# GpSimd splits the attention weights in the middle of the expert loop: a drain between two of its instructions becomes a wait on the first one's semaphore

## The chip, the cores and the metric

One core of a Trainium2 chip runs the whole program. The metric is the device time of one execution in microseconds (us); lower is better. The profile's names are PE (TensorE), DVE (VectorE), ACT (ScalarE), POOL (GpSimd) and SP (SyncE); an engine name with a small q (POOLq) is that engine's sequencer, which carries out waits, semaphore increments and drains.

## The reference, cut to what matters

The input is 4 sequences of 1024 tokens with 512 features. Three layers follow one another:

```
x = x + 0.5 * ffn(layernorm(x))      # 32 routed experts, top 6, capacity 192, plus one shared expert
x = x + attention(layernorm(x))      # 4 query heads on 1 key/value head of 128, causal, rotary
x = x + 0.5 * ffn(layernorm(x))      # the same weights again
```

An expert gathers its 192 tokens, computes `silu(x Wg) * (x Wu)`, multiplies by `Wd` (inner width 256), weights each row and adds the rows back to their tokens. Products are made to fp32 accuracy from two parts of each factor: hi is the value cast to fp32r, lo is value minus hi. The attention layer needs its weights `w_qkv` (512 x 768) and `w_out` (512 x 512) in this form too. They are split while the experts of the first ffn run, and that splitting is what the change touches.

## The kernel before, in words

`ffn(0)`, `attention` and `ffn(1)` run one after the other. Inside an ffn, `front` does the normalisation, shared expert and routing; `routed_experts` then loops over the 32 experts with everything double buffered (`u = e % 2`). No planner orders the expert loop: each engine has its own list of instructions, written out by hand, and semaphores tie the lists together.

For expert e the work passes through the engines like this:

- SP loads the expert's weights `e_raw` (1.5 MB) as soon as the buffer is free, that is when DVE has finished the lo part of expert e-2 (L881 in the first half, L890 in a loop).
- POOL gathers the expert's tokens with two indirect DMAs, `gather`, L898 (`e_xg` from the table `htab`).
- PE turns the tokens (L1100), which waits for the gathers to land. It then computes gate and up (L1111, L1112) and down (L87 to L89). It turns expert e+2 before it computes gate and up of e+1.
- ACT casts the weights to `e_w_hi` (L958), unloads PSUM, and writes the weighted result `e_y` in `weigh` (L987 and L990). `weigh` of expert e waits until `y_free` has reached e+1.
- DVE subtracts `e_w_lo` (L1032) and does the other lo parts and sums.
- POOL adds the result rows into the output with two indirect DMAs, `scatter`, L909. The scatter of an expert waits for its `e_y`, and for `added`, which says that all earlier scatters have landed. It increments `y_free` (L906) before it issues.

POOL issues all of this from one list. For each index e it runs `gather_next(e)`, which waits for `col_done` and gathers the tokens of expert e+2, and then the scatter of expert e-2. In the first ffn, for the ten indices e = 4 to 13, a `split_chunk` stands between them:

```
for e in range(4, 4 + chunks):
    gather_next(e // 2, e % 2)
    split_chunk(e - 4)
    scatter(e // 2 - 1, e % 2)
```

A chunk is 128 x 512 fp32 (256 KB). `attention_chunks` lists six of `w_qkv` and four of `w_out`. The first six are loaded by SP before the expert loop, and the other four are loaded by L885 behind the expert weights. Chunk c waits for its load, is cast to hi (L915), the drain follows (L916), and the subtraction gives lo (L917). The second ffn has the same loop without chunks.

Of the kernel before, what the change touches and what calls it, by code (L numbers as in the profile page):

```python
# [31 lines left out]
XS = 6  # L32
# [63 lines left out]
def own_semaphore(nc, k, name):  # L96

    k.ffn_semaphores.append(nc.alloc_semaphore(name=name))
    return k.ffn_semaphores[-1]
# [720 lines left out]
def routed_experts(nc, a, k, n, htab, acc, slots, raw, xs, w_loaded, y_stored):  # L820

    with ExitStack() as ctx:
        sb = lambda name, shape, dt: ctx.enter_context(nc.sbuf_tensor(f"{name}{n}", shape, dt))
        pb = lambda name: ctx.enter_context(nc.psum_tensor(f"{name}{n}", [P, 512], F32))
        sem = lambda name: own_semaphore(nc, k, f"{name}{n}")
# [29 lines left out]
        d_ready, y_ready = sem("e_d_ready"), sem("e_y_ready")  # L855
        part = lambda t, c, m: t[:, 2 * c:2 * c + 2, m, :]
        if n == 0:
            att_loaded, att_split = [sem(f"e_att_loaded{u}_") for u in range(XS)], sem("e_att_split")
            cut = lambda ap, c: ap.rearrange("p k c -> p (k c)")[:, c * D:(c + 1) * D]
            attention_chunks = [tuple(cut(ap, c) for ap in (hi[:, :, :], lo[:, :, :], from_))  # L860
                                for hi, lo, from_, size in ((k.wqkv_hi, k.wqkv_lo, a["w_qkv"], WQKV),
                                                            (k.wo_hi, k.wo_lo, a["w_out"], H * D))
                                for c in range(size // D)]
# [4 lines left out]
        with nc.Block() as block:  # L868

            @block.sync  # L870
            def _(sp):
                if n == 0:
                    for c, (hi, lo, from_) in enumerate(attention_chunks):
                        if c < XS:
                            sp.wait_ge(y_stored[c], 16 * ((NT - 1 - c) // XS + 1))
                            sp.dma_start(xs[c][:, :], from_).then_inc(att_loaded[c], 16)
                for i in range(E // 4):
                    for u in range(2):
                        e = 2 * i + u
                        sp.wait_ge(lo_ready, 3 * e + 3)  # L880
                        sp.dma_start(raw[u][:, :], a["w_experts"][e + 2, :, :]).then_inc(w_loaded[u], 16)  # L881
                        if n == 0 and XS <= e - 4 + XS - 1 < len(attention_chunks):
                            c = e - 4 + XS - 1
                            sp.wait_ge(att_split, c - XS + 1)
                            sp.dma_start(xs[c % XS][:, :], attention_chunks[c][2]).then_inc(att_loaded[c % XS], 16)  # L885
                with sp.Fori(E // 4, E // 2 - 1) as i:
                    for u in range(2):
                        e = 2 * i + u
                        sp.wait_ge(lo_ready, 3 * e + 3)
                        sp.dma_start(raw[u][:, :], a["w_experts"][bass.ds(e + 2, 1), :, :].rearrange("o p c -> p (o c)")).then_inc(w_loaded[u], 16)  # L890

            @block.gpsimd
            def _(pool):
                pool.sem_inc(y_free, 2)

                def gather(u):
                    for q in range(2):
                        pool.indirect_dma_start(xg[u][q][:, :], None, htab,  # L898
                                                bass.IndirectOffsetOnAxis(ap=gather_idx[u][:, q:q + 1], axis=0)).then_inc(gathered[u], 16)

                def scatter(i, u, first=False):
                    e = 2 * i + u
                    pool.wait_ge(y_ready, 2 * e + 2 + 2)
                    if not first:
                        pool.wait_ge(added, 32 * e)
                        pool.sem_inc(y_free, 1)  # L906
                    pool.sem_inc(seen, 1)  # L907
                    for q in range(2):
                        pool.indirect_dma_start(acc, bass.IndirectOffsetOnAxis(ap=add_idx[u][:, q:q + 1], axis=0),  # L909
                                                y[u][q][:, :], None, compute_op=ALU.add).then_inc(added, 16)  # L910

                def split_chunk(c):
                    hi, lo, from_ = attention_chunks[c]
                    pool.wait_ge(att_loaded[c % XS], 16 * (c // XS) + 16)
                    pool.tensor_copy(hi, xs[c % XS][:, :])  # L915
                    pool.drain()  # L916
                    pool.tensor_tensor(lo, xs[c % XS][:, :], hi.bitcast(F32), ALU.subtract).then_inc(att_split, 1)  # L917

                def gather_next(i, u):
                    pool.wait_ge(col_done, 2 * i + u + 1)  # L920
                    pool.sem_inc(seen, 1)
                    gather(u)

                for u in range(2):
                    pool.tensor_copy(gather_idx[u][:, :], slots[:, 2 * u:2 * u + 2])
                pool.drain()
                gather(0)
                gather(1)
                gather_next(0, 0)
                gather_next(0, 1)  # L930
                for u in range(XS):
                    pool.wait_ge(y_stored[u], 16 * ((NT - 1 - u) // XS + 1))
                gather_next(1, 0)
                scatter(0, 0, first=True)
                gather_next(1, 1)
                scatter(0, 1)
                chunks = len(attention_chunks) if n == 0 else 0
# [4 lines that stand above are left out]
                with pool.Fori((4 + chunks) // 2, E // 2 - 1) as i:  # L942
                    for u in range(2):
                        gather_next(i, u)
                        scatter(i - 1, u)
                for i in (E // 2 - 2, E // 2 - 1):
                    for u in range(2):
                        scatter(i, u)
                pool.wait_ge(added, 32 * E)
# [716 lines left out]
def build_program(nc, a, out):  # L1666
    with ExitStack() as ctx:
        k = allocate_kept(nc, ctx)
        htab = nc.dram_tensor("htab", [ROWS, ROW], F32).ap()
        x1 = nc.dram_tensor("x_after_ffn", [ROWS, D], F32).ap()  # L1670
        x2 = nc.dram_tensor("x_after_attention", [TOK, D], F32).ap()

        def ffn(n, src, acc):
            with nc.sbuf_tensor(f"slots{n}", [HALF, 2 * E + 4], U32) as slots, ExitStack() as places:
                staged = [staged_buffers(nc, places, "place", PLACES - 2 + u, n) for u in range(2)]
                raw = [nc.alloc_sbuf_tensor_at(f"e_raw{u}_{n}", [P, WALL], F32, offset=staged[u][0]) for u in range(2)]
                xs = [places.enter_context(nc.sbuf_tensor(f"d_xs{u}_{n}", [P, D], F32)) for u in range(XS)]
                w_loaded = [own_semaphore(nc, k, f"e_w_loaded{u}_{n}") for u in range(2)]
                y_stored = [own_semaphore(nc, k, f"d_y_stored{u}_{n}") for u in range(XS)]
                front(nc, a, k, n, src, acc, (x1, out), htab, slots, staged, raw, xs, w_loaded, y_stored)  # L1680
                routed_experts(nc, a, k, n, htab, acc, slots, raw, xs, w_loaded, y_stored)

        ffn(0, a["x"], x1)
        attention(nc, a, k, x1, x2)
        ffn(1, x2, out)
# [72 lines left out]
```

## Time and profile before

| quantity | value |
|---|---|
| time, median of 3 runs | 1744.37 us (1742.22 to 1751.76) |
| profiled execution: own time | 1754.33 us |
| profiled execution: span | 1752.5 us |
| mean granted TensorE clock, share of full speed | 0.945 |
| PE, DVE, ACT, POOL busy, share of the span | 86%, 64%, 59%, 45% |

The span is the profiler's time from first to last instruction; the execution's own time is 1.8 us longer. The shares are averages over stages that are limited by different things, so the stage in which the change stands has to be read by itself. The expert loop of the first ffn lies between about 219 us and 600 us of the span, with the ten chunks between 271.7 and 408.3 us.

### The profile page before, as it was taken

Reading aid. Unit: us, or ns where it says so; the run is one execution under the profiler, and the core shown is the slowest. Engines: PE = TensorE matmul, PEld = TensorE weight load, DVE = VectorE, ACT = ScalarE, POOL = GpSimd, SP = SyncE. Lnnn points to the kernel's source line nnn. Section 1 sums busy time; section 2 is a strip of 40 time slices with the busy share of each in tenths; the row PEclk is TensorE's granted clock in tenths of the full one; section 3 lists DMA queues with packets and bytes.
Section 4 is the critical chain, followed back from the end, with each engine's and each line's share of the span. In section 5 each row is a group of like instructions: output and inputs, shape, how many; then the busy total and the mean of one; then the engine's idle time right before and its main releaser. Section 6 shows DMA issues by size and latency. Waiting matters only on the chain. (4 is left out here: it accounts for less than half of the span.)

```text
span 1752.5 us, 26196 instructions
## 1 busy us (share of the span) xinstructions
PE 1508.2 (86%) x8434; PEld 1255.1 (72%) x8436; DVE 1113.4 (64%) x2274; ACT 1027.8 (59%) x2098; POOL 788.7 (45%) x679
## 2 busy tenths in 40 slices
PE   5999867777899278999999999986999969999994
PEld 4877766666787266887888788774777758787773
DVE  5669756445677236676766676664558867777773
ACT  5852346445677237666766766653763437777773
POOL 0113145555555266656665556520113234565553
PEclk9999979888999779999999999998999989999998
DMA  7745467656898410111111111103664447999994
GB/s 263 253 126 174 121 197 224 175 163 184 240 263 247 74 48 25 53 45 46 40 37 61 49 37 37 43 30 112 228 217 137 145 139 225 258 262 259 258 258 78
DMA packets 94597, 255.57 MB, mean 146 GB/s; under 512 B 19152, under 2 KB 20112, under 8 KB 86192
## 3 DMA queue, kind: packets, MB, share of 16 engines
q1 hardware_dynamic: 71984, 202.58, 34.4%
q0 software_dynamic: 22528, 51.92, 14.6%
q8 instruction: 45, 0.74, 0.2%
q14 instruction: 40, 0.33, 0.1%
HBM read 185.70 MB, written 68.76 MB: 145 GB/s over the span
## 5 line engine op out<-in xcount | busy, mean ns | idle before, releaser
L1032 DVE TENSOR_TENSOR e_w_lo<-e_raw,e_w_hi 128x1024 fp32r<-128x1024 f32 x192 | 234.8, 1224 | 158.9 <-ACT e_w_hi L958 142.3
L958 ACT ACTIVATE e_w_hi<-e_raw 128x1024 fp32r<-128x1024 f32 x192 | 202.4, 1055 | 34.6 <-PEq L270 20.8
L1537 POOL TENSOR_SCALAR t_prob<-t_prob,t_inv 128x128 f32<-128x128 f32 (+7 forms) x128 | 111.8, 874 | 222.9 <-DVE t_inv L1444 222.9
L1111 PE MATMUL e_ps_gate<-e_xt,e_w_hi 128*128 128x384 f32 x512 | 177.9, 407 | 20.3 <-DVE e_w_lo L1032 20.1
L898 POOL DMA_INDIRECT e_xg<-htab,e_gather_idx x128 | 146.5, 1145 | 65.0 <-issue 39.0
L909 POOL DMA_INDIRECT out<-e_y,e_add_idx x64 | 102.0, 1593 | 113.8 <-DMA out<-e_y,e_add_idx 90.3
L1111 PE MATMUL e_ps_up<-e_xt,e_w_hi 128*128 128x384 f32 x512 | 152.9, 363 | 0.0
L353 POOL TENSOR_SCALAR d_inter<-d_inter 128x512 f32<-128x512 f32 x32 | 26.2, 818 | 268.8 <-DVE d_inter L518 268.7
L909 POOL DMA_INDIRECT x_after_ffn<-e_y,e_add_idx x64 | 102.2, 1597 | 92.7 <-DMA x_after_ffn<-e_y,e_add_idx 62.9
L1100 PE MATMUL e_ps_t<-ident,e_xg 96*128 96x96 f32 x512 | 63.2, 274 | 91.3 <-DMA e_xg<-htab,e_gather_idx 90.7
L1112 PE MATMUL e_ps_gate<-e_xt,e_w_lo 128*128 128x192 f32 x512 | 138.6, 271 | 0.0
L1339 ACT ACTIVATE t_prob<-a_wide,t_neg_max,a_q_scale 128x128 f32<-128x128 f32 (+7 forms) x128 | 106.4, 832 | 53.8 <-DVE t_neg_max L1438 53.5
L1100 PEld LDWEIGHTS e_ps_t<-ident,e_xg 96*128 96x128 f32 x512 | 53.9, 157 | 111.1 <-issue 84.4
L1112 PE MATMUL e_ps_up<-e_xt,e_w_lo 128*128 128x192 f32 x512 | 129.7, 253 | 0.0
L1111 PEld LDWEIGHTS e_ps_gate<-e_xt,e_w_hi 128*128 128x128 f32 x512 | 108.9, 213 | 27.3 <-issue 15.2
L1346 ACT ACTIVATE t_pt<-a_bank 128x512 fp32r<-128x512 f32 x144 | 84.0, 596 | 68.5 <-PE a_bank L1614 68.3
L1449 DVE TENSOR_TENSOR t_pt<-a_bank,t_pt 128x512 fp32r<-128x512 f32 x144 | 96.2, 684 | 42.0 <-ACT t_pt L1346 41.3
L1112 PEld LDWEIGHTS e_ps_gate<-e_xt,e_w_lo 128*128 128x128 f32 x512 | 110.2, 215 | 0.0
L87 PE MATMUL e_ps_down<-e_w_hi,e_in_hi 128*96 128x512 f32 x256 | 101.1, 395 | 2.9 <-ACT e_y L990 2.9
L89 PE MATMUL e_ps_down<-e_w_hi,e_in_lo 128*96 128x512 f32 x256 | 101.5, 396 | 0.0
L88 PE MATMUL e_ps_down<-e_w_lo,e_in_hi 128*96 128x512 f32 x256 | 100.2, 392 | 0.0
L1112 PEld LDWEIGHTS e_ps_up<-e_xt,e_w_lo 128*128 128x128 f32 x512 | 98.7, 193 | 0.0
(222 smaller groups left out, 4577.1 us busy)
## 6 DMA issues: line engine op xcount, KB each, us to landing
e_raw<-in_w_experts SPq DMA_DIRECT2D x64, 1536.0 KB
htab<-d_h SPq DMA_DIRECT2D x16, 1024.0 KB, 5.2
d_x<-in_x SPq DMA_DIRECT2D x16, 512.0 KB, 6.8
d_xs<-in_x SPq DMA_DIRECT2D x32, 256.0 KB, 3.6
x_after_ffn<-d_xs SPq DMA_DIRECT2D x32, 256.0 KB, 3.1
q_x<-x_after_ffn SPq DMA_DIRECT2D x32, 256.0 KB, 3.0
t_res<-x_after_ffn SPq DMA_DIRECT2D x32, 256.0 KB, 2.6
x_after_attention<-t_res SPq DMA_DIRECT2D x32, 256.0 KB, 2.0
```

The costliest lines, as they stand in the source:

```text
L87: pe.matmul(out, wh, mh, start=first, stop=False)
L88: pe.matmul(out, wh, ml, start=False, stop=False)
L89: return pe.matmul(out, wl, mh, start=False, stop=last)
L898: pool.indirect_dma_start(xg[u][q][:, :], None, htab, bass.IndirectOffsetOnAxis(ap=gather_idx[u][:, q:q + 1], axis=0)).then_inc(gathered[u ...
L909: pool.indirect_dma_start(acc, bass.IndirectOffsetOnAxis(ap=add_idx[u][:, q:q + 1], axis=0), y[u][q][:, :], None, compute_op=ALU.add).then ...
L958: act.activation(w_hi[u][:, cols], raw[u][:, cols], ACT.Copy).then_inc(hi_ready, 1)
L1032: dve.tensor_tensor(w_lo[u][:, cols], raw[u][:, cols], w_hi[u][:, cols].bitcast(F32), ALU.subtract).then_inc(lo_ready, 1)
L1100: got = pe.transpose(ps_t[c][:, at:at + HALF], xg[u][q][:, (2 * c + b) * P:(2 * c + b + 1) * P], k.ident[0:HALF, 0:HALF])
L1111: pe.matmul(out, w[0][:, c, cols], xt[u][:, c, :, :], start=c == 0, stop=False)
L1112: got = pe.matmul(out[:, 0:CAP], w[1][:, c, cols], xt[u][:, c, 0, :], start=False, stop=c == KB - 1)
L1339: act.activation(prob[:, u, 0:width(i)], ps_s[i % 2][:, 0:width(i)], ACT.Exp, scale=q_scale[:, i // H % QSLOTS, i % H:i % H + 1], bias=neg ...
L1537: pool.tensor_scalar(prob[:, u, 0:width(i)], prob[:, u, 0:width(i)], inv[:, u:u + 1], 1.0, ALU.mult, ALU.mult).then_inc(p_ready, 1)
```

## The change

The cast now increments a new semaphore, `att_hi`. In place of the drain, POOL waits until `att_hi` has reached c+1, so it waits for this cast alone. Nothing else is changed: the same instructions run in the same order.

```diff
         if n == 0:
-            att_loaded, att_split = [sem(f"e_att_loaded{u}_") for u in range(XS)], sem("e_att_split")
+            att_loaded, att_hi, att_split = ([sem(f"e_att_loaded{u}_") for u in range(XS)], sem("e_att_hi"),
+                                              sem("e_att_split"))
...
                 def split_chunk(c):
                     hi, lo, from_ = attention_chunks[c]
                     pool.wait_ge(att_loaded[c % XS], 16 * (c // XS) + 16)
-                    pool.tensor_copy(hi, xs[c % XS][:, :])
-                    pool.drain()
+                    pool.tensor_copy(hi, xs[c % XS][:, :]).then_inc(att_hi, 1)
+                    pool.wait_ge(att_hi, c + 1)
                     pool.tensor_tensor(lo, xs[c % XS][:, :], hi.bitcast(F32), ALU.subtract).then_inc(att_split, 1)
```

## Rows read from the trace of the kernel before

**Rows 1.** Windows: busy us of each engine, then PEclk, DMA share, GB/s.

```profile
276.81:407.05 130.24, 91.50 (x474) 80.63 (x473) 66.58 (x114) 63.75 (x111) 75.43 (x55) 0.83 0.65 183
431.24:562.05 130.81, 117.58 (x730) 101.96 (x728) 92.15 (x165) 92.75 (x164) 73.48 (x56) 0.99 0.88 247
```

**Rows 2.** Waits of PE, ACT and DVE, 276 to 407: total us, times, longest.

```profile
PE e_ps_t L1100 <- DMA e_xg<-htab,e_gather_idx: 37.7, 9, 5.7
...
ACT e_add_idx L987 <- POOLq L906: 34.1, 8, 6.0
...
DVE e_w_lo L1032 <- ACT e_w_hi L958: 52.2, 13, 7.9
```

**Rows 3.** Timeline of POOL, one chunk cycle: start us, length us, then the instruction.

```profile
307.38 1.26 POOL L917 TENSOR_TENSOR wqkv_lo<-d_xs,wqkv_hi 128x512 fp32r<-128x512 f32 x1 [5.61 <-issue]
308.81 1.48 POOL L909 DMA_INDIRECT x_after_ffn<-e_y,e_add_idx  x1 [0.16 <-issue]
310.59 1.98 POOL L909 DMA_INDIRECT x_after_ffn<-e_y,e_add_idx  x1 [0.31 <-issue]
312.88 1.47 POOL L898 DMA_INDIRECT e_xg<-htab,e_gather_idx  x1 [0.30 <-issue]
314.65 1.93 POOL L898 DMA_INDIRECT e_xg<-htab,e_gather_idx  x1 [0.31 <-issue]
316.58 0.62 POOL L915 CAST wqkv_hi<-d_xs 128x512 fp32r<-128x512 f32 x1
321.98 1.27 POOL L917 TENSOR_TENSOR wqkv_lo<-d_xs,wqkv_hi 128x512 fp32r<-128x512 f32 x1 [4.77 <-issue]
```

**Rows 4.** Timeline of PE: the turn after that cycle's gathers.

```profile
321.81 0.88 PE L1100 MATMUL e_ps_t<-ident,e_xg 96*128 96x96 f32 x8 [3.55 <-DMA e_xg<-htab,e_gather_idx]
```

**Rows 5.** Timeline of POOL in attention: an instruction behind the drain of L1519.

```profile
931.77 1.72 POOL L1522 TENSOR_TENSOR q_by_sin<-q_gained,a_sin 128x320 f32<-128x320 f32 x2 [0.16 <-issue]
```

**Rows 6.** Timeline of PE and POOL: a turn and its gathers, no drain between.

```profile
414.25 1.30 POOL L898 DMA_INDIRECT e_xg<-htab,e_gather_idx  x1 [0.30 <-issue]
...
420.92 0.42 PE L1100 MATMUL e_ps_t<-ident,e_xg 96*128 96x96 f32 x1 [5.76 <-DMA e_xg<-htab,e_gather_idx]
```

**Rows 7.** Timeline of POOL: first scatter instructions, before, across and behind the chunks.

```profile
265.45 1.52 POOL L909 DMA_INDIRECT x_after_ffn<-e_y,e_add_idx  x1 [4.22 <-DMA x_after_ffn<-e_y,e_add_idx]
...
420.69 1.46 POOL L909 DMA_INDIRECT x_after_ffn<-e_y,e_add_idx  x1 [5.14 <-DMA x_after_ffn<-e_y,e_add_idx]
...
431.24 1.71 POOL L909 DMA_INDIRECT x_after_ffn<-e_y,e_add_idx  x1 [4.44 <-DMA x_after_ffn<-e_y,e_add_idx]
...
562.05 1.47 POOL L909 DMA_INDIRECT x_after_ffn<-e_y,e_add_idx  x1 [3.92 <-DMA x_after_ffn<-e_y,e_add_idx]
```

**Rows 8.** Timeline of POOL, second ffn: the scatters of experts 1 and 12.

```profile
1469.38 2.56 POOL L909 DMA_INDIRECT out<-e_y,e_add_idx  x1 [5.33 <-DMA out<-e_y,e_add_idx]
...
1571.70 1.47 POOL L909 DMA_INDIRECT out<-e_y,e_add_idx  x1 [3.14 <-DMA out<-e_y,e_add_idx]
```

**Rows 9.** Waits of POOL, 420 to 565 us.

```profile
POOL x_after_ffn L909 <- DMA x_after_ffn<-e_y,e_add_idx: 49.5, 14, 5.1
```

**Rows 10.** Timeline of POOL: the longest chunk cycle without its drain.

```profile
393.12 1.26 POOL L917 TENSOR_TENSOR wo_lo<-d_xs,wo_hi 128x512 fp32r<-128x512 f32 x1 [4.65 <-issue]
...
402.30 0.96 POOL L915 CAST wo_hi<-d_xs 128x512 fp32r<-128x512 f32 x1
```

**Rows 11.** Timeline of POOL in the front: a subtraction behind an ACT cast.

```profile
133.00 3.15 POOL L356 TENSOR_TENSOR d_in_lo<-d_inter,d_in_hi 128x512 fp32r<-128x512 f32 x1 [0.75 <-ACT d_in_hi L418]
```

**Rows 12.** One line's instructions, whole program: ns min/median/max, first and last start.

```profile
L917 POOL TENSOR_TENSOR wqkv_lo<-d_xs,wqkv_hi x6: 1265/1270/1282, 276.8 to 351.4; 128x512 fp32r<-128x512 f32 x6
...
L1032 DVE TENSOR_TENSOR e_w_lo<-e_raw,e_w_hi x192: 1206/1223/1921, 219.6 to 1724.6; 128x1024 fp32r<-128x1024 f32 x192
...
L909 POOL DMA_INDIRECT x_after_ffn<-e_y,e_add_idx x64: 1407/1465/2554, 255.2 to 593.2; - x64
...
L898 POOL DMA_INDIRECT e_xg<-htab,e_gather_idx x128: 916/963/2065, 219.8 to 1705.4; - x128
```

## The prediction

> **What bounds the kernel now.** I read the stage around the change first in the windows view, because the page's shares average over stages. The two windows of some 130 us lie in the same expert loop, the first over the chunks, the second behind them [rows 1]. The first holds nine of POOL's cycles, the second 14, so an expert costs 130.24 / 9 = 14.47 us with chunks and 130.81 / 14 = 9.34 us without. In the first window PE is busy 70% of the time, and no engine and no DMA queue is full (DMA share 0.65). In the second PE is busy 90% and the DMA engines 88%. So the chunk stage waits for something that is no unit's capacity.
>
> The waits view says for what. PE waits 37.7 us for the gathers. ACT waits 34.1 us for the sequencer of POOL at L906, the `y_free` increment just behind the chunk's subtraction. DVE waits 52.2 us for ACT, so that is the same wait passed on [rows 2]. All of them wait for POOL's list.
>
> The timeline of POOL shows the hole [rows 3]. The cast ends at 316.58 + 0.62 = 317.20 and the subtraction starts at 321.98, 4.77 us later, with "issue" as the reason: nothing in the profile but the drain stands there. Each of the ten chunks has such a hole, here of 5.61 and 4.77 us, further on of 4.65 us [rows 3, 10]. What does the drain wait for? PE's turn, which waits for those gathers to land, starts at 321.81 [rows 4], 0.16 us before the subtraction. I found this same distance of 0.16 to 0.17 us at nine of the ten chunks (at the other PE was busy with older work). In attention, where POOL has no DMA under way, what stands behind a drain starts after 0.16 us [rows 5]. I read it so: the drain lets POOL go on only when its own gathers have landed.
>
> Is it perhaps the gathers that wait for the drain? The gathers at 414.25 have no drain behind them. Their issue ends at 415.55 and the turn starts at 420.92, 5.37 us later [rows 6]; with the drain it was 321.81 - 316.58 = 5.23 us. The landing takes as long without a drain, so the drain follows it.
>
> This closes a loop that runs through POOL alone: subtraction 1.27, scatters and gathers with their gaps, landing 5.2, next subtraction. From 307.38 to 321.98 that is 14.60 us, about the 14.47 us of the mean. The expert's whole time in this stage is this loop.
>
> **The change part by part.** *The drain goes.* The loop falls open: the gathers may land while POOL subtracts and scatters. The whole hole is not simply subtracted, since other limits wait below. There are two.
>
> The first is POOL's own work. In the chunk window it is busy 75.43 us, or 8.38 us a cycle, and the gaps between its instructions are 0.16 + 3 x 0.30 = 1.06 us, so 9.44 us [rows 1, 3]. Another value comes from behind the chunks, where POOL works 73.48 / 14 = 5.25 us a cycle [rows 1]; with three gaps of 0.30, a subtraction of 1.27, the cast of 0.62 to 0.96 and two gaps of 0.16 this gives 8.4 to 8.7 us. The longest recorded cycle without its drain runs from 393.12 to 402.30 + 0.96 = 403.26, 10.14 us [rows 10].
>
> The second limit is what makes 9.34 us behind the chunks: each scatter waits there for the landing of the one before, 49.5 us in 14 waits, 3.5 us each [rows 9], with PE and DMA close to full. This 3.5 us is the cover for the added POOL work of about 2.3 us (cast, subtraction, gaps). Without cover it would cost 10 x 2.3 = 23 us.
>
> *The wait comes.* Ten waits on the cast's semaphore. No row shows POOL waiting for its own semaphore. From below I take the 0.16 us of a drain with nothing to wait for [rows 5]. From above I take 0.75 us, the time in which ACT hears of a POOL instruction, casts, and POOL hears of ACT [rows 11]. The value is 0.16, nearest in kind, since cast and wait are on one engine; the other end makes 6 us over the ten. Queued behind the wait are the subtraction, the `y_free` increment for ACT and the scatter for PE's next results; all of these waited for the drain until now. The Trainium skill, Perfetto Trace Analysis, section GPSIMD Engine Instruction, says that for an instruction that writes, the profile's end is the point at which the last of the cores has its bytes acknowledged and the semaphore is updated. By it the wait ends with the recorded cast plus propagation, as in the sum. The nine coincidences are no test of this, because there the drain held everything.
>
> *The semaphore* itself costs nothing more: an increment rides on the cast.
>
> *The cycle that follows.* POOL's 9.44 + 0.16 = 9.60 us and the landing loop's 9.34 us are close, and they vary separately, so the longer of the two decides in each cycle. I take 9.8 us. The one step behind the last chunk has no chunk: 9.34. Four chunks of 262 KB are still to be loaded in this stage; at 247 GB/s [rows 1] that is 1.06 us each, 4.2 us at most if the DMA engines are full. They are full to 0.88, so I take 2.
>
> *The sum.* From the scatter at 265.45 to that at 420.69 lie 11 steps and 155.24 us [rows 7]. Afterwards they are 10 x 9.8 + 9.34 + 2 = 109.3 us. The gain is 46 us. A check: the same 11 steps in the second ffn, which has no chunks, take 1571.70 - 1469.38 = 102.3 us [rows 8], and 14 steps behind the chunks take 130.8 us [rows 7]. Against the second ffn alone the gain would be 53 us. Nothing gives the gain back later: the rest of the loop runs at 9.34 us either way, and attention starts behind the last scatter and moves forward as a whole. PE's granted clock should rise too: 0.83 of full speed with chunks, a mixture of its two levels (1.2 and 2.4 GHz) with PE idle for up to 5.7 us ahead of a turn, against 0.99 behind them [rows 1, 2]. It is contained in the 9.34 us.
>
> In the profiled execution that is 1752.5 - 46 = 1706.5 us of span and 1754.3 - 46 = 1708 us of time. That execution lies 10 us above the median of the runs. I carry the gain over unchanged to the median: 1744.4 - 46 = **1698 us**.
>
> **The rivals.** *A, the forecast: the landing wait disappears.* For it: the nine coincidences, the drain of 0.16 us without DMAs, the control at 414.25.
>
> *B, no effect.* The cast's semaphore might be updated only when everything POOL issued earlier is complete, the DMAs too, as the drain does. Then the subtraction stays behind the landing and the time is 1744 us. For it: no row shows a waiter on a POOL compute instruction while gathers are under way. Against it: the cast is recorded as ended after 0.62 to 0.96 us [rows 3, 10], long before the landing.
>
> *C, contention takes part of the gain.* So far all subtractions of L917 take 1265 to 1282 ns [rows 12], but they ran while DVE stood idle for ACT. Afterwards they run beside DVE's `e_w_lo` of 1.22 us, three for each expert. The same subtraction took 3.15 us in one case in the front [rows 11], where DVE was at work. If each takes 3.15, POOL's cycle is 9.60 + 1.88 = 11.5 us and the 11 steps take 115 + 9.3 + 2 = 126 us: gain 29, time 1715 us. Against it: the casts and the DMA issues of the loop already lie beside a busy DVE and are in the 8.38 us. The Trainium skill, SBUF — State Buffer, section SBUF: two separate sides, says that a DVE instruction with two SBUF inputs and a GpSimd instruction that reads SBUF exclude each other for a whole instruction. By it a subtraction would wait up to one DVE instruction, and this speaks for C; the rows show 3.15 as the exception, the median of such subtractions in the front being 1.29 us.
>
> *D, slower.* The same contention at its full size, on POOL's DMA issues as well. If each scatter takes its longest 2.55 us, each gather its longest 2.07 us [rows 12], the subtraction 3.15 and the cast 0.96, and the wait 0.75, the cycle is 3.15 + 0.16 + 5.1 + 4.14 + 0.9 + 0.96 + 0.75 = 15.2 us, and with DVE's three `e_w_lo` each at the longest 1.92 instead of 1.22 some 2.1 us more where POOL waits for ACT and DVE: 17.3 us. That would be (17.3 - 14.1) x 10 = 32 us slower, 1776 us (14.1 is 155.24 / 11). It decides against the change from a cycle of 15.0 us on. Against it: behind the chunks, with DVE 70% busy, POOL's cycle is 6.2 us, far from these maxima.
>
> **How the numbers follow.** A gets 0.76, B 0.12, C 0.09, D 0.03. Within A the bounds are 11 x 9.34 = 102.7 us (gain 52.5, time 1692) and ten of the longest cycles, 10 x (10.14 + 0.16) + 9.34 + 4.2 = 116.5 us (gain 39, time 1706). The wait at 0.75 would add 6. The median of before is itself uncertain by some 4 us. So the range is 1688 to 1720 us: it takes in A with its unknown costs and C, and leaves out B and D with 0.15. Half a percent, about what a measurement of this kernel can tell from no change, is 8.7 us; A and C are faster by more (0.85), B is the same (0.12), D is slower (0.03).
>
> **What the profile afterwards would show.** Step one, the drain's wait: the idle time before L917 falls from about 5 us to under 1 us, and the subtraction starts several us before PE's turn of the same gathers. Step two, the loop: L909 in the chunk stage waits again for the landing of the scatter before, or for nothing; the scatters follow one another at 9.3 to 10.1 us; ACT's wait for L906 is nearly gone. Step three: PEclk near 0.97 and a DMA share near 0.88 in the stage, which ends near 375 us instead of 421. B would show the holes where they were. C would show L917 well above 1.3 us. The prediction is wrong if the cast's semaphore is late, or if the chunk cycle meets a limit above 12 us that the present loop hides.

## The result, and the profile after

| | before | after |
|---|---|---|
| time, median (range) | 1747.04 us (1742.22 to 1751.76, 4 runs) | 1697.82 us (1692.4 to 1698.78, 4 runs) |
| profiled execution: span, time | 1752.5, 1754.33 us | 1695.4, 1697.18 us |
| mean granted clock | 0.945 | 0.959 |

The ratio of after to before is 0.9694, with a 95% interval of 0.9656 to 0.9733. A second measurement of the changed kernel gave 0.9694 again (0.967 to 0.9718). The forecast was 1698 us.

Line numbers behind the edit are one higher in the kernel after: the cast is L916, the subtraction L918, the scatter L910, the gather L899.

POOL's timeline shows one cycle of the chunk stage, from one subtraction to the next. It answers to [rows 3].

```profile
291.82 1.29 POOL L918 TENSOR_TENSOR wqkv_lo<-d_xs,wqkv_hi 128x512 fp32r<-128x512 f32 x1
293.28 2.34 POOL L910 DMA_INDIRECT x_after_ffn<-e_y,e_add_idx  x1 [0.17 <-DVE e_gather_idx L1046]
295.93 1.45 POOL L910 DMA_INDIRECT x_after_ffn<-e_y,e_add_idx  x1 [0.30 <-issue]
297.68 1.29 POOL L899 DMA_INDIRECT e_xg<-htab,e_gather_idx  x1 [0.30 <-issue]
299.28 0.96 POOL L899 DMA_INDIRECT e_xg<-htab,e_gather_idx  x1 [0.30 <-issue]
300.24 1.54 POOL L916 CAST wqkv_hi<-d_xs 128x512 fp32r<-128x512 f32 x1
301.86 1.29 POOL L918 TENSOR_TENSOR wqkv_lo<-d_xs,wqkv_hi 128x512 fp32r<-128x512 f32 x1
```

The hole is gone. By these rows the cast ends at 301.78 and the subtraction starts at 301.86, 0.08 us later: that is what the wait on the semaphore costs. The cycle takes 301.86 - 291.82 = 10.04 us, and no gap in it is longer than 0.30 us. POOL goes from one instruction to the next without waiting for anybody. PE's turn behind the same gathers starts 3.2 us after the subtraction, where it started 0.16 us before it in [rows 4]:

```profile
305.04 0.82 PE L1101 MATMUL e_ps_t<-ident,e_xg 96*128 96x96 f32 x8
```

The windows view, with the columns of [rows 1], has the steady part of the chunk stage and then ten steps behind it.

```profile
283.25:363.52 80.27, 68.38 (x420) 59.74 (x419) 61.78 (x97) 53.10 (x96) 70.98 (x48) 0.98 0.88 251
371.69:463.40 91.71, 84.57 (x529) 73.30 (x528) 68.26 (x126) 67.78 (x122) 55.33 (x40) 1.00 0.91 263
```

The first window holds 8 steps, 10.03 us each, of which POOL is busy 70.98 / 8 = 8.87 us; with 1.06 us of gaps between instructions and the 0.1 us of the wait this is the whole step. The clock granted to PE has risen from 0.83 to 0.98, so nearly all of the stage is at 2.4 GHz and no longer a mixture with 1.2 GHz; PE no longer stands idle for 5 us in each step.

The waits of PE and ACT from 265 to 375 us answer to [rows 2].

```profile
PE e_ps_gate L1112 <- DVE e_w_lo L1033: 14.2, 9, 1.8
...
ACT e_silu L977 <- DVE e_gate_sum L1050: 21.3, 12, 2.1
```

PE's 37.7 us for the gathers and ACT's 34.1 us for POOL's sequencer are gone from the list. What is left for these two engines are short waits of at most 2.1 us, most of them for DVE.

The scatter starts of POOL's timeline give the sum's terms, as [rows 7] do for before.

```profile
262.92 1.49 POOL L910 DMA_INDIRECT x_after_ffn<-e_y,e_add_idx  x1 [4.26 <-DMA x_after_ffn<-e_y,e_add_idx]
...
371.69 1.46 POOL L910 DMA_INDIRECT x_after_ffn<-e_y,e_add_idx  x1 [1.22 <-DMA x_after_ffn<-e_y,e_add_idx]
```

The 11 steps take 108.77 us; they took 155.24 us. The forecast for them was 109.3 us. (A step is the distance from the first scatter instruction of one expert to that of the next.)

### The profile page after: what moved, and what is told of

It reads as the page before. It is cut to its first block and busy times, and to the rows that moved or that the text cites. A ratio compares the mean times of both kernels' runs of the same rounds, so it can differ in the third digit from the quotient of the medians.

```text
span 1695.4 us, 26186 instructions
## 1 busy us (share of the span) xinstructions
PE 1486.7 (88%) x8434; PEld 1235.5 (73%) x8436; DVE 1116.9 (66%) x2274; ACT 1023.5 (60%) x2098; POOL 794.0 (47%) x679
## 5 line engine op out<-in xcount | busy, mean ns | idle before, releaser
L1112 PE MATMUL e_ps_gate<-e_xt,e_w_hi 128*128 128x384 f32 x512 | 163.7, 382 | 39.1 <-DVE e_w_lo L1033 38.9
L899 POOL DMA_INDIRECT e_xg<-htab,e_gather_idx x128 | 140.3, 1096 | 63.6 <-issue 47.0
L910 POOL DMA_INDIRECT out<-e_y,e_add_idx x64 | 99.2, 1550 | 114.8 <-DMA out<-e_y,e_add_idx 92.1
L910 POOL DMA_INDIRECT x_after_ffn<-e_y,e_add_idx x64 | 109.6, 1712 | 82.5 <-DMA x_after_ffn<-e_y,e_add_idx 55.3
L1112 PEld LDWEIGHTS e_ps_gate<-e_xt,e_w_hi 128*128 128x128 f32 x512 | 100.3, 196 | 49.0 <-issue 27.5
L1113 PE MATMUL e_ps_gate<-e_xt,e_w_lo 128*128 128x192 f32 x512 | 132.4, 259 | 0.0
L1113 PEld LDWEIGHTS e_ps_gate<-e_xt,e_w_lo 128*128 128x128 f32 x512 | 101.8, 199 | 0.0
L1112 PEld LDWEIGHTS e_ps_up<-e_xt,e_w_hi 128*128 128x128 f32 x512 | 96.8, 189 | 0.0
L1437 DVE TENSOR_REDUCE t_top<-a_wide 128x1 f32<-128x128 f32 (+7 forms) x128 | 95.5, 746 | 1.4 <-PE a_wide L1607 1.4
```

What stands on the lines that cost most here:

```text
L899: pool.indirect_dma_start(xg[u][q][:, :], None, htab, bass.IndirectOffsetOnAxis(ap=gather_idx[u][:, q:q + 1], axis=0)).then_inc(gathered[u ...
L1112: pe.matmul(out, w[0][:, c, cols], xt[u][:, c, :, :], start=c == 0, stop=False)
L1113: got = pe.matmul(out[:, 0:CAP], w[1][:, c, cols], xt[u][:, c, 0, :], start=False, stop=c == KB - 1)
```

## The experiments

The theory to be tested has two parts. Part one: the drain lets POOL go on only when the DMAs that POOL itself issued have landed. Part two: with the drain gone, POOL's own work is the limit of the chunk stage. All edits are against the changed kernel unless the text says otherwise.

**Drain and semaphore together.**

```diff
                     pool.wait_ge(att_hi, c + 1)
+                    pool.drain()
                     pool.tensor_tensor(lo, ...)
```

> The changed kernel with the drain put back behind the new wait, so both stand between cast and subtraction. Theory 1 (the drain lets POOL go on only when its own DMAs have landed): the holes of about 5 us before the subtraction return and the subtraction starts 0.16 us after PE's turn; the 11 scatter steps take about 155 us again, time about 1747 us. Rival (the drain was slow only because the cast was unfinished when it came): with the wait in front the drain costs 0.16 us, time about 1698 us.

Measured: 1746.97 us median of 8 runs, 0.9997 of the kernel before (0.9968 to 1.0026). The whole gain is undone by the drain alone. The trace has the drain as an instruction of POOL's sequencer. Here it starts with the cast finished, so nothing of the cast is in its length. The first row below is its record (ns min/median/max); then come POOL's timeline and PE's at the fifth chunk.

```profile
L918 POOLq DRAIN  x10: 4010/5000/6728, 272.8 to 403.3; - x10
```

```profile
337.40 1.27 POOL L919 TENSOR_TENSOR wqkv_lo<-d_xs,wqkv_hi 128x512 fp32r<-128x512 f32 x1 [5.43 <-issue]
```

```profile
337.24 0.49 PE L1102 MATMUL e_ps_t<-ident,e_xg 96*128 96x96 f32 x2 [4.94 <-DMA e_xg<-htab,e_gather_idx]
```

The drain takes 4.0 to 6.7 us behind a finished cast, and the distance of 0.16 us to PE's turn is back. The 11 steps take 156.15 us, expected were about 155. The rival, an unfinished cast, falls.

**The drain ahead of the cast.**

```diff
+                    pool.drain()
                     pool.tensor_copy(hi, xs[c % XS][:, :]).then_inc(att_hi, 1)
                     pool.wait_ge(att_hi, c + 1)
```

> The changed kernel with a drain ahead of the cast, right behind the gathers, and the semaphore wait kept behind the cast. Theory 1: the hole of about 5 us moves in front of the cast, which starts 0.16 us after PE's turn; the cycle grows by the cast of 0.6 to 0.9 us to about 15.2 us, since the cast no longer lies inside the landing; time 1750 to 1756 us. Rival (what is slow is draining the cast): the drain costs 0.16 us, time about 1700 us.

Measured: 1755.11 us, one run. POOL's timeline shows the hole in its new place, and PE's turn of the same gathers lies 0.15 us before the cast.

```profile
324.40 0.61 POOL L917 CAST wqkv_hi<-d_xs 128x512 fp32r<-128x512 f32 x1 [6.41 <-issue]
325.09 1.27 POOL L919 TENSOR_TENSOR wqkv_lo<-d_xs,wqkv_hi 128x512 fp32r<-128x512 f32 x1
...
340.32 0.61 POOL L917 CAST wqkv_hi<-d_xs 128x512 fp32r<-128x512 f32 x1 [6.76 <-issue]
```

```profile
324.25 0.58 PE L1102 MATMUL e_ps_t<-ident,e_xg 96*128 96x96 f32 x2 [5.77 <-DMA e_xg<-htab,e_gather_idx]
```

The ten steps take 15.3 us on average (416.89 - 264.00 = 152.9 for ten), as expected 15.2. The drain does not need a cast before it.

**The drain where there are no chunks.** In the loop of the second ffn:

```diff
                         gather_next(i, u)
+                        if n == 1:
+                            pool.drain()
                         scatter(i - 1, u)
```

> The changed kernel with a drain between gathers and scatter in the loop of the second ffn, where no chunk, cast or subtraction of POOL exists; 26 steps have it. Theory 1: each step becomes a loop of two scatters, two gathers and their landing, 1.46 + 1.43 to 1.98 + 0.96 to 1.47 + 0.96 to 1.9 plus gaps of 1.2 plus 5.4 = 11.4 to 13.4 us instead of 9.3, so 55 to 105 us slower than 1698: 1753 to 1803 us. Rival (the drain is slow only behind a cast): 26 drains of 0.16 us hidden under the wait for the scatter before, 1698 us.

Measured: 1795.25 us, 1.0273 of the kernel before (1.0201 to 1.0345, two runs), so about 97 us slower than the changed kernel's 1697.82. POOL's timeline:

```profile
1492.05 1.46 POOL L910 DMA_INDIRECT out<-e_y,e_add_idx  x1 [5.90 <-issue]
1493.81 2.44 POOL L910 DMA_INDIRECT out<-e_y,e_add_idx  x1 [0.30 <-issue]
1496.56 1.47 POOL L899 DMA_INDIRECT e_xg<-htab,e_gather_idx  x1 [0.30 <-issue]
1498.33 1.91 POOL L899 DMA_INDIRECT e_xg<-htab,e_gather_idx  x1 [0.30 <-issue]
1505.21 1.47 POOL L910 DMA_INDIRECT out<-e_y,e_add_idx  x1 [4.97 <-issue]
```

A step is 13.2 us here and 13.4 us on average (1438.75 to 1559.04 for nine), against 9.3 us without the drain. With no cast and no subtraction of POOL anywhere near, 26 drains cost 26 x 4.07 = 106 us by the steps, close to the 97 us by the time. A drain behind GpSimd's own DMA issues costs its 4 us with or without a split beside it.

**Other DMAs under the drain.** Against the kernel before, so with the drain:

```diff
                 for e in range(4, 4 + chunks):
+                    split_chunk(e - 4)
                     gather_next(e // 2, e % 2)
-                    split_chunk(e - 4)
                     scatter(e // 2 - 1, e % 2)
```

> The kernel before, drain kept, with the chunk's split moved ahead of the gathers, so that the DMAs under way at the drain are the two scatters of the step before. Theory 1: the subtraction starts when those scatters have landed, 6 to 7.4 us behind their issue; the gathers are issued behind it; cycle 13.4 to 15 us, time 1735 to 1752 us, and PE's turn no longer coincides with the subtraction but follows it by 7 to 8 us. Rival (a fixed price of about 5 us): subtraction 5 us behind the cast, cycle about 14.4 us too, but without relation to the landing of the scatters.

Measured: 1737.25 us, one run. This is the sharpest test, because the landing time of the scatters varied. POOL's timeline at a short and at a long drain:

```profile
279.98 1.45 POOL L909 DMA_INDIRECT x_after_ffn<-e_y,e_add_idx  x1 [0.30 <-issue]
280.95 2.14 POOL L915 CAST wqkv_hi<-d_xs 128x512 fp32r<-128x512 f32 x1
284.53 1.50 POOL L917 TENSOR_TENSOR wqkv_lo<-d_xs,wqkv_hi 128x512 fp32r<-128x512 f32 x1 [1.45 <-DVE e_gather_idx L1045]
...
314.33 2.22 POOL L909 DMA_INDIRECT x_after_ffn<-e_y,e_add_idx  x1 [0.30 <-issue]
316.08 1.10 POOL L915 CAST wqkv_hi<-d_xs 128x512 fp32r<-128x512 f32 x1
324.05 1.47 POOL L917 TENSOR_TENSOR wqkv_lo<-d_xs,wqkv_hi 128x512 fp32r<-128x512 f32 x1 [6.88 <-issue]
```

The DMA view of narrow windows gives the time from issue to landing of these two scatters, 4.2 and 9.4 us (the last number of each row).

```profile
x_after_ffn<-e_y,e_add_idx POOLq DMA_INDIRECT x1, 4.2
...
x_after_ffn<-e_y,e_add_idx POOLq DMA_INDIRECT x1, 9.4
```

The subtraction follows at 279.98 + 4.2 + 0.35 = 284.53 and at 314.33 + 9.4 + 0.32 = 324.05. Nine of the ten steps have such a row, with landings of 4.2, 4.2, 4.3, 9.4, 7.3, 7.4, 8.6, 7.4 and 7.3 us, and each time the subtraction starts about 0.3 us behind the landing. So the hole is no fixed price: it is as long as the landing is late. (The "DVE" named as releaser in the third row is a coincidence in time; that copy of DVE releases nothing here.) PE's turn starts 8.0 and 6.3 us behind these two subtractions, so the drain does not wait for PE either.

Does the drain wait for POOL's own DMAs alone, or for every DMA under way? The kernel before can't tell: at the end of its drain at 321.98 no DMA engine moves anything. Here one can. SP issues a chunk load at 283.03 that lands 8.4 us later, near 291.4, and the drain is over at 284.53. The first two rows below are SP's timeline and the DMA view of 283:284.53, the last two the DMA view of 284.53:285.0. The queue that still moves data there is not POOL's (POOL's is the software queue).

```profile
283.03 0.43 SPq L885 DMA_DIRECT2D d_xs<-in_w_out  x1
d_xs<-in_w_out SPq DMA_DIRECT2D x1, 256.0 KB, 8.4
...
DMA packets 10, 0.12 MB, mean 261 GB/s; under 512 B 0, under 2 KB 0, under 8 KB 0
q1 hardware_dynamic: 10, 0.12, 81.0%
```

So POOL's drain does not wait for the loads of SP. Part one stands.

**More work for POOL.** The chunk is cast a second time, into `lo`, which the subtraction then overwrites:

```diff
                     pool.tensor_copy(hi, xs[c % XS][:, :]).then_inc(att_hi, 1)
-                    pool.wait_ge(att_hi, c + 1)
+                    pool.tensor_copy(lo, xs[c % XS][:, :]).then_inc(att_hi, 1)
+                    pool.wait_ge(att_hi, 2 * c + 2)
```

> The changed kernel with a second cast of the same size for each chunk (into lo, which the subtraction then overwrites). Theory 1 (POOL is full in the stage): each of the ten steps grows by that cast, 0.6 to 1.5 us, so 6 to 15 us slower than 1698: 1704 to 1713 us. Rival (the landing of scatters, DMA or PE limit the stage and POOL has room): 1698 us.

Measured: 1705.26 us (1703.34 to 1710.25), 0.9744 of before (0.97 to 0.9788). The 11 steps take 377.77 - 263.61 = 114.16 us, 5.4 us more than 108.77. The time is 7.4 us above the changed kernel's first median, with overlapping intervals of the ratio. It lies at the low edge of the expectation, and the steps lie below it (5.4 us, expected 6 to 15). The ten steps are of two kinds. In the last six (304.89 to 370.51) POOL has no idle time and a step takes 10.94 us, 0.9 more than 10.03: there POOL's own work is the limit, as expected. In the first four a step takes 10.3 us, and POOL has idle time of 1.2 to 2.3 us ahead of the scatter:

```profile
304.89 2.40 POOL L910 DMA_INDIRECT x_after_ffn<-e_y,e_add_idx  x1 [2.29 <-issue]
```

The profile names no releaser. But the code has only two waits there, for `e_y` and for `added`, and ACT had finished every `e_y` 3.4 to 4.6 us before these four scatters. What is left is `added`, the landing of the scatter before, 8.1 to 8.8 us behind its second instruction. So POOL's work and the landing loop are close together in this stage, and a small shift decides which of them limits a step.

**No split among the experts.** The splits stand behind the last scatter, and the four chunk loads of L886 are left out of the stage too. Only the stage is read.

```diff
-                        if n == 0 and XS <= e - 4 + XS - 1 < len(attention_chunks):
+                        if False:
...
                     gather_next(e // 2, e % 2)
-                    split_chunk(e - 4)
                     scatter(e // 2 - 1, e % 2)
...
+                for c in range(chunks):
+                    split_chunk(c)
                 pool.wait_ge(added, 32 * E)
```

> The changed kernel without any split among the experts: all ten chunks are split behind the last scatter, and the last four chunks are not loaded (the first four are split in their place, so the results of the attention are those of other weights). Only the stage is read. Theory 1: the 11 scatter steps take 102 to 104 us instead of 108.8, like the second ffn's 102.3, and the scatters wait for the landing of those before. Rival (DMA or PE limit the stage): 108 us. The time of the whole gains the 5 to 7 us and loses up to 25 us at the end, where POOL works alone: 1700 to 1718 us.

Measured: 1704.46 us, one run. The windows view of the 11 steps:

```profile
264.67:366.00 101.33, 94.58 (x590) 81.53 (x590) 75.03 (x139) 75.16 (x135) 58.05 (x45) 1.00 0.91 260
```

101.33 us instead of 108.77 (expected 102 to 104), with PE busy 93% and the DMA engines 91%. So the split and its four loads together still cost 7 us in this stage. The run does not divide them; by the prediction's own estimate the loads can be up to 4.2 us of it. What lies below is again the landing loop. POOL has idle time ahead of each of the 11 scatters, and ACT had finished its `e_y` 2.9 to 5.2 us before, which leaves `added`. Here ACT's row and POOL's for one of them:

```profile
297.37 1.24 ACT L992 ACTIVATE e_y<-e_ps_down,e_wcol 96x512 f32<-96x512 f32 x2
303.80 1.46 POOL L910 DMA_INDIRECT x_after_ffn<-e_y,e_add_idx  x1 [3.74 <-issue]
```

Whether the landing would come earlier with PE and the DMA engines less full was not tested.

**Contention with DVE.** The subtraction of `e_w_lo` is replaced:

```diff
-                    dve.tensor_tensor(w_lo[u][:, cols], raw[u][:, cols], w_hi[u][:, cols].bitcast(F32),
-                                      ALU.subtract).then_inc(lo_ready, 1)
+                    dve.memset(w_lo[u][:, cols].bitcast(F32), 0.0).then_inc(lo_ready, 1)
```

> The changed kernel in which DVE fills e_w_lo with zeros instead of subtracting (the lo parts of the expert weights are left out), so DVE no longer reads two SBUF inputs beside POOL's work. Only durations in the stage are read. Theory 1 with contention: the cast falls from 1.54 to about 0.62 us and the first scatter from 2.35 to about 1.46 us, POOL's step from 10.03 to 8.2 to 8.6 us, and the step becomes 9.0 to 9.5 us, limited by the landing or by PE. Rival (these durations have nothing to do with DVE's reads): cast 1.54, scatter 2.35 and step 10.0 us as before.

Measured: 1684.96 us, one run. POOL's timeline, one step:

```profile
292.05 1.48 POOL L910 DMA_INDIRECT x_after_ffn<-e_y,e_add_idx  x1 [2.21 <-issue]
293.83 1.51 POOL L910 DMA_INDIRECT x_after_ffn<-e_y,e_add_idx  x1 [0.30 <-issue]
...
297.89 0.62 POOL L916 CAST wqkv_hi<-d_xs 128x512 fp32r<-128x512 f32 x1
298.59 1.30 POOL L918 TENSOR_TENSOR wqkv_lo<-d_xs,wqkv_hi 128x512 fp32r<-128x512 f32 x1
```

The cast is 0.62 or 0.63 us in all ten steps instead of 1.54, the first scatter 1.48 instead of 2.35, and the first gather 0.96 to 1.01 instead of 1.29. The subtraction of POOL stays at 1.28 to 1.33. POOL is busy 6.8 us a step, where it was 8.87, so its work falls under the next limit: ten steps take 355.06 - 263.68 = 91.4 us, 9.14 each, with idle time again ahead of most scatters. So 0.9 us of the cast, 0.9 us of the scatter and 0.3 us of the gather were DVE's two-input subtraction. The Trainium skill, SBUF — State Buffer, section SBUF: two separate sides, says that such an instruction and a GpSimd instruction that reads SBUF exclude each other; the trace agrees, with 1.54 against 0.62 us for the cast. That the DMA issue is prolonged as well, by 0.87 us, is shown by these runs alone. A caution: the run also frees time on DVE, so the 9.14 us of the step are not POOL's relief alone.

**Half chunks.** A version meant to beat both: each chunk in two halves of 256 columns, one half in each of 20 steps. L886's reloads wait for two increments per chunk.

```diff
-                def split_chunk(c):
-                    hi, lo, from_ = attention_chunks[c]
+                def split_half(j):
+                    c, cols = j // 2, slice(j % 2 * D // 2, (j % 2 + 1) * D // 2)
+                    hi, lo = (t[:, cols] for t in attention_chunks[c][0:2])
...
-                chunks = len(attention_chunks) if n == 0 else 0
+                chunks = 2 * len(attention_chunks) if n == 0 else 0
```

> The changed kernel with each chunk split in two halves of 256 columns, one half in each of 20 steps instead of a whole chunk in each of 10. Theory 1 (POOL's own work is the limit of the chunk stage at 10.03 us a step, the landing of the scatters at about 9.3 us everywhere else): the added work falls to about 1.3 us a step, fits under the idle time of 3.5 us, and the 20 steps run at 9.3 to 9.5 us: 10 x 0.7 = 7 us less than 1698, at most 2 of it lost again: 1691 to 1694 us. Rival (the stage is limited by DMA, which was 88% busy, or by PE): no change, 1698 us. Second rival (contention, more instructions on POOL beside DVE): 1700 us or more.

Measured: 1693.35 us (1690.12 to 1697.21, 6 runs), 0.9677 of before (0.9643 to 0.9711). I repeated it beside the changed kernel on the same chip, since 4 us are less than one such interval.

> The changed kernel itself, timed beside the version with half chunks on the same chip. Both theories: 1692 to 1700 us, ratio to the kernel before 0.968 to 0.972.

> The version with half chunks again, beside the changed kernel on the same chip. If POOL's own work is the limit of the chunk stage: 3 to 7 us less than the changed kernel. If the first result's 4 us were chance: within 2 us of it.

Measured: changed kernel 1694.89 us (1692.21 to 1699.26), 0.9694 (0.967 to 0.9718); half chunks 1692.24 us (1688.29 to 1698.89), 0.9669 (0.9646 to 0.9692). The medians differ by 2.65 us in the expected direction, which is less than the 3 to 7 us of the theory and more than the 2 us of chance; the intervals overlap. In the traces the first 11 steps take 106.0 and 104.1 us against 108.8 and 108.5 us, so the steps have become shorter as expected, but less: 9.5 to 9.6 us, not 9.3. The half cast takes 1.1 us in most steps and 0.4 us in the others, so halving the chunk does not halve its price. Whether the version is faster in the whole, by 2 to 4 us, stays open.

**The order of split and gathers, with the semaphore.** The same exchange of two lines as above, in the changed kernel:

> The changed kernel with the chunk's split moved ahead of the gathers (the order of the earlier experiment, but with the semaphore in place of the drain). If POOL's own work is the limit: same instructions, same sum, 10 us a step, 1694 to 1702 us. Rival (the order against DVE's work decides how long POOL's instructions take, or the gathers come too late for PE): more than 5 us away from 1698 in either direction.

Measured: 1701.18 us (1698.04 to 1701.9), 0.9716 (0.9695 to 0.9736). The median is 6.3 us above that of the changed kernel beside it, with overlapping intervals of the ratio; the 11 steps take 114.13 us, 5.6 us more. The time lies inside the expectation and the step does not: 10.4 us instead of 10. POOL's waits, 270 to 370 us:

```profile
POOL x_after_ffn L910 <- DMA x_after_ffn<-e_y,e_add_idx: 17.8, 10, 2.3
```

Here the scatter waits 1.8 us per step for the landing of the scatter before. The expectation of the same sum was wrong: POOL is busy 83.16 us in these 11 steps, where it was 93.27 in the changed kernel, mainly because the first scatter is back at 1.46 to 1.71 us in all the steps and no longer 2.35. POOL has less to do and the step is longer all the same. So in this order the landing is the limit, not POOL's work:

```profile
304.72 1.46 POOL L910 DMA_INDIRECT x_after_ffn<-e_y,e_add_idx  x1 [2.34 <-DMA x_after_ffn<-e_y,e_add_idx]
```

The landing lies 8.3 to 9.1 us behind the start of the second scatter instruction before it. In the steady steps of the changed kernel it is at most 7.4 us, since the next scatter starts there without waiting for it. Why the landing is later in this order was not tested.

## Why the prediction was right

**Step one, what the drain waits for: right.** Four experiments show it: 4.0 to 6.7 us behind a finished cast, 6 us ahead of the cast, 4 us a step with no cast at all, and a hole that follows landings from 4.2 to 9.4 us with a constant 0.3 us, while a load of SP is still under way. Rival B (the cast's semaphore comes only with the landing) is refuted by the result: the wait ends 0.08 us behind the cast, at 301.86, only 1.6 us behind the end of the gathers' issue at 300.24, while their landing took 5.2 us before. Rival D, all of POOL's instructions at their longest, did not come about.

**The price of the wait: small, as forecast, but below its range.** Taken as 0.16 us from [rows 5], which was also the lower bound, measured 0.08 us. Over ten chunks that is 0.8 us.

**POOL's cycle as the next limit: right, and its size close.** Forecast 9.6 us with the wait and 9.8 us per step, measured 10.03 us with no idle time left. POOL is busy 8.87 us a step instead of 8.38; that is 0.5 us of added contention, of which the cheaper wait gives 0.1 back. The 8.38 us taken from the trace before held contention already, since POOL is busy only 6.8 us a step without DVE's subtraction; this is why the sum came so close. What changed is where it falls: the cast takes 1.54 us where [rows 3, 10] had 0.62 to 0.96, and the first scatter 2.35 us. Rival C, in which contention takes part of the gain, was thus real in kind, but sat in other instructions than it said. It had the subtraction at 3.15 us; this stayed at 1.29 in nine of ten steps (one 2.17), and the cast and the scatter paid instead.

**The landing loop as the limit below: right.** Without any split the stage takes 101.3 us for 11 steps, against 102.7 in the lower bound, and the scatters wait for landings, by elimination. In the order with the split ahead it sets all the steps, at 10.4 us; the forecast took its 9.34 us as fixed, and it is not.

**The stage: right, its parts less exactly.** 155.24 - 108.77 = 46.5 us, forecast 46. The ten steps with a chunk took 100.6 us, forecast 98 and 2 for the chunk loads; the one without took 8.17 us, forecast 9.34. The sum agrees to 0.6 us because these misses are of opposite sign. No run shows the 2 us of the loads by themselves.

**The whole: a little more than forecast, and the exact hit is luck.** The gain in time is 49 us by the first medians and about 55 us by the second measurement; the ratio of 0.9694 stands against 1698.4 / 1744.4 = 0.9736 forecast, which is just outside the interval. That the time came out at 1698 all the same is luck: the median of before that I subtracted from, 1744.37 us, was low (1747.04 with one run more, 1750.15 in the second measurement), and the gain was too small by about as much. The 57.1 us between the two profiled spans divide into 2.5 us ahead of the stage, 46.5 in it, 3.3 in the rest of the loop and 4.8 behind the last scatter. The forecast put all but the stage at nothing ("the rest of the loop runs at 9.34 us either way"). Whether the change gained any of it is not shown. The part from the 12th scatter to the last took 168.2 to 172.3 us in the four profiles with a drain beside the chunks, and 167.1 to 168.0 us in six of those with the semaphore alone, but 171.2 us in the run with a second cast. What comes behind the last scatter varies by 11 us between the profiles (1150.5 to 1161.2 us), without regard to the drain. It stays open how the last 3 to 9 us divide.

## What to carry to other kernels

A drain on GpSimd waits not only for the instruction before it, but until the gathers and scatters that GpSimd issued have landed. Other engines that issue DMAs were not tried. Between two dependent instructions of GpSimd, in a loop with gathers or scatters, put a semaphore on the first one: it cost 0.08 us here where the drain cost 4 to 7 us, and 26 needless drains in a loop without any such pair cost 97 us. Look for such a drain where an engine stands idle with "issue" as the reason while another engine's wait for a DMA ends at the same moment. And when a stall goes, add up the work of the engine that it stood on: that was the next limit here, with the landing of the scatters less than 1 us a step below it. Where the profile says "issue" in front of an instruction for which the code has several waits, rule them out one by one; that is how the landing was found there.

## What the runs showed that I had not expected

- The contention between POOL and DVE works in both directions. With POOL's split beside it, DVE's copy of the gather indices takes 0.89 us in the steps at 292.25 and 302.29, where its median over the program before is 0.155 us. Both times it ends 0.03 us behind POOL's subtraction (293.14 and 293.11, 303.18 and 303.15). One of the three `e_w_lo` of an expert takes 1.54 us instead of 1.22. DVE's timeline after:

```profile
299.76 1.55 DVE L1033 TENSOR_TENSOR e_w_lo<-e_raw,e_w_hi 128x1024 fp32r<-128x1024 f32 x1 [1.62 <-ACT e_w_hi L959]
...
302.29 0.89 DVE L1046 COPY e_gather_idx<-slots 96x2 uint32 x1
```

- The stage locks into a fixed pattern. From 283.25 to 363.52 us eight steps in a row take 10.03 us each, and the same instructions collide with DVE in each of them. A shift in the pattern changes which instruction is prolonged: with half chunks, where the cast takes 0.4 us POOL's subtraction sometimes takes 1.7 instead of 0.74.
- The landing of a scatter varied from 4.2 to 9.4 us within 40 us of one run, the one with the split ahead and the drain. It goes with the start of SP's 1.5 MB weight load: the load is issued 2.7 us behind the scatters of 290.92 and 302.97, which land after 4.2 and 4.3 us, and within 1 us of those of 314.33 and 330.14, which take 9.4 and 7.3 us. No run changes the load alone. Two of SP's rows:

```profile
293.60 0.33 SPq L881 DMA_DIRECT2D e_raw<-in_w_experts  x1
...
315.27 0.33 SPq L881 DMA_DIRECT2D e_raw<-in_w_experts  x1
```
